# Constant matmuls ahead of five waits on TensorE, and a later X+U on GpSimd, in a 16-batch hybrid layer

## The reference

```python
x = x + attention(layernorm(x), Wqkv, Wproj)        # 16 heads of 16, rotary embedding, causal softmax
x = x + ffn(layernorm(x), weight, bias)             # blocks of 32 rounded to an FP6 E2M3 grid, then x @ W.T + bias
x = x + mamba_and_mlp(layernorm(x), ...)            # see below
x = x + ffn(layernorm(x), weight, bias)
```

## Time and profile before

| what | value |
|---|---|
| median of 3 runs | 9802.93 us (9801.65 to 9804.70) |
| the profiled execution | 9804.51 us |
| its span (first to last instruction) | 9802.8 us |
| mean granted TensorE clock | 0.909 |
| PE busy | 7878.8 us (80%) |
| DVE busy | 7618.6 us (78%) |
| POOL busy | 4330.9 us (44%) |
| ACT busy | 4259.3 us (43%) |

### The profile page before, as it was taken

One profiled execution on the slowest core, in us unless ns is written; L12 is line 12 of the kernel. 1 busy time (PEld: TensorE's weight loads), 2 busy tenths in 40 slices (PEclk: granted clock), 3 DMA queues, 4 the chain that ended last, 5 costly groups with the idle time before them and its releaser, 6 DMA issues. The chain is left out here.

```text
span 9802.8 us, 98275 instructions
## 1 busy us (share of the span) xinstructions
PE 7878.8 (80%) x31796; PEld 3811.3 (39%) x31796; DVE 7618.6 (78%) x11589; ACT 4259.3 (43%) x7991; POOL 4330.9 (44%) x2631
## 2 busy tenths in 40 slices
PE   5788787887978878788887878878788787887977
PEld 2343343433434334343343434434343243432434
DVE  5787977779687696876878778787787877878777
ACT  2535435254442543525435254353534535345353
POOL 1451825418154271632726336262361724518245
PEclk8898998989989898898989889899898988989989
DMA  3020020200202002020020200102011020100202
GB/s 78 1 51 3 5 49 1 52 1 9 45 0 53 1 9 45 0 53 1 13 41 0 53 1 22 32 0 53 1 28 26 0 53 1 38 15 5 49 1 52
DMA packets 265191, 229.93 MB, mean 23 GB/s; under 512 B 26947, under 2 KB 237635, under 8 KB 264531
## 3 DMA queue, kind: packets, MB, share of 16 engines
q1 hardware_dynamic: 264678, 223.50, 10.6%
HBM read 151.60 MB, written 70.25 MB: 23 GB/s over the span
## 5 line engine op out<-in xcount | busy, mean ns | idle before, releaser
L639 POOL TENSOR_TENSOR arena<-arena 128x1024 f32<-128x1024 f32 x1024 | 2435.6, 2389 | 1312.4 <-DVE arena L1041 862.4
L778 ACT ACTIVATE PS<-arena,Aneg 128x512 f32<-128x512 f32 x2048 | 1410.5, 691 | 1628.1 <-DVE XNT L1081 883.6
L704 ACT ACTIVATE arena<-PS 128x512 f32<-128x512 f32 (+3 forms) x3072 | 1286.9, 508 | 861.4 <-PE PS L1249 856.9
L1363 PE MATMUL PS<-XNT,identf 128*128 128x512 f32 x2048 | 1012.2, 618 | 320.9 <-POOL XNT L622 320.9
L948 DVE TENSOR_REDUCE pm<-PS 128x1 f32<-128x512 f32 (+3 forms) x1728 | 1051.2, 663 | 271.5 <-PE PS L1228 169.6
L601 POOL TENSOR_SCALAR_AFFINE_SELECT arena<-arena 128x512 f32<-128x512 f32 x512 | 329.6, 644 | 2063.6 <-ACT arena L704 2063.6
L1225 PE MATMUL PS<-arena 96*128 96x512 bf16 (+3 forms) x3072 | 1105.5, 385 | 106.3 <-PEq L1447 49.4
L1363 PE MATMUL PS<-arena,identf 128*128 128x512 f32 x2048 | 1025.6, 625 | 161.9 <-DVE arena L1057 161.9
L1249 PE MATMUL PS<-arena 99*128 99x512 bf16 (+3 forms) x3072 | 894.5, 332 | 5.9
L1348 PE MATMUL PS<-arena,sel 96*128 96x512 bf16 x1664 | 513.7, 391 | 389.0 <-DVE arena L1057 319.5
L686 ACT ACTIVATE XNT<-PS 128x512 f32<-128x512 f32 x320 | 187.4, 597 | 1335.2 <-PE PS L1184 1334.5
(11 more groups left out here) (143 smaller groups left out, 13086.2 us busy)
## 6 DMA issues: line engine op xcount, KB each, us to landing
pieces_scratch<-arena SPq DMA_DIRECT2D x816, 64.0 KB
arena<-pieces_scratch SPq DMA_DIRECT2D x68, 384.0 KB, 10.0
arena<-pieces_scratch SPq DMA_DIRECT2D x85, 256.0 KB, 10.5
arena<-in_x SPq DMA_DIRECT2D x17, 1024.0 KB, 5.6
U<-in_x SPq DMA_DIRECT2D x17, 1024.0 KB, 5.6
arena<-pieces_scratch SPq DMA_DIRECT2D x136, 128.0 KB, 10.2
out<-X SPq DMA_DIRECT2D x64, 256.0 KB, 5.7
arena<-pieces_scratch SPq DMA_DIRECT2D x17, 768.0 KB
```

Of the source, the lines that this page charges most:

```text
L639: nc.gpsimd.tensor_tensor(DB[:, n % 2], DTU[:, j, half(th)].unsqueeze(1).to_broadcast([P, SP2, TH]), BB[:, SP2 * sg:SP2 * (sg + 1), :], AL ...
L704: A(PT[s % len(PT)][:, hh, 0:w], bank(t_bank(n))[:, 0:w], ACT.Exp, scale=DH ** -0.5)\
L778: A(bank(da_bank(m)), DT[:, j, half(th)], ACT.Exp, scale=Aneg[:, j, SP2 * sg + ss:SP2 * sg + ss + 1]).then_inc(S("dA"), 1)
L1363: ins = MM(bank(4 + jt % 2), identf[:, :], HS[k % len(HS)][:, ss, :], start=False, stop=sg == NSG - 1 and ss == SP2 - 1)
```

## The change

`keep_busy(b, count)` issues `count` matmuls of the constants `identf` (the 128 x 128 identity, as weights) and `wproj[:, 0, :]` (256 columns) into bank b. Nothing reads what they write: the next use of the bank starts it anew. They stand ahead of waits in five places: the half `th` = 1 of both quantized layers (10 and 14 of them), ahead of `turn(2)` (5), ahead of x_proj's third and fourth `xc` (4 and 3), and in steps 0 and 1 of the scan loop (6, 2 and 4). Together that is 48 per batch, 96 matmul instructions. On POOL, X+U gets one more wait, `fxn` >= 8, the last of `front_norm`'s tiles.

```diff
             pool.wait_ge(S("R"), 2 * NT)
+            pool.wait_ge(S("fxn"), NT)
             nc.gpsimd.tensor_tensor(X[:, :, :], X[:, :, :], U[:, :, :], ALU.add).then_inc(S("xu"), 1)
...
+            def keep_busy(b, count):
+                for _ in range(count):
+                    MM(bank(b)[:, 0:C], identf[:, :], wproj[:, 0, :], start=True, stop=True)
...
             def quant_products(f):
                 rnd = (1, 4)[f]
                 for th in range(NTH):
+                    if th:
+                        keep_busy(NT // NTH, (10, 14)[f])
                     turn(rnd, lambda p, tt: quant_rows(f, p)[:, tt, :], "xd", lambda p: f * NT // 2 + p + 1,
...
+            keep_busy(7, 5)
             turn(2, lambda p, tt: RM[0][2 * p + tt], "R", lambda p: 2 * p + 2)
...
                 for j in range(ND):
+                    if th == 0 and j >= 2:
+                        keep_busy(5, (4, 3)[j - 2])
                     pe.wait_ge(S("xc"), j + 1)
...
                     jt, th, j, sg = m_unit(n)
+                    if n < 2:
+                        keep_busy(5, (6, 2)[n])
                     if b_copied(n + 1):
                         spread_b(b_copied(n + 1))
+                    if n == 1:
+                        keep_busy(5, 4)
                     if spread_c(n):
```

## The result

| | before | changed |
|---|---|---|
| median | 9803.77 us (4 runs) | 9586.55 us (4 runs, 9584.89 to 9598.34) |
| ratio | | 0.978, 95% interval 0.977 to 0.980 |
| profiled execution, its span | 9804.5, 9802.8 us | 9585.7, 9583.9 us |
| mean granted clock | 0.909 | 0.937 |
| PE busy | 7878.8 us | 7974.4 us |

The kernel is 217 us faster; 9606 us were forecast, with a range of 9560 to 9690. The 1536 added matmul instructions are all in the trace, and PE's busy time rises by 96 us only: the rest of its work runs faster.

A forecast was written before the change was run, and what follows sets the result against it. No engine was full; PE at 0.50 on chains and X+U's collision with `front_norm` cost time. Terms 1.3 + 1.3 + 0.6 + 2.4 + 5.1 + 1.8 = 12.5 us, taken as 12.3, over sixteen passes: 197 us, 9606 us; range 9560 to 9690.

The forecast's parts named there:

- The low clock lies on chains: At six places PE's clock falls to 0.50 while another engine soon waits for PE; half the covered low time comes back.
- the prediction's three sights: Low clock follows PE's idle time; another engine soon waits for PE in all six places; X+U and `front_norm` collide.
- X+U: On POOL, X+U waiting for `front_norm` removes PE's 3.53 us wait and the low stretch behind it: 5.1 us a pass.
- rival (d): X+U blocks DVE's silu products instead of the norm; its 5.1 us are lost, 9685 us; chance 0.05.
- The loop's block ends late: In the scan loop the block behind the wait for `z` is 1.1 us too long; 0.2 us charged.
- PE's waits for `xd`: Sign in the profile after: PE waits 1 us or less for `xd` ahead of the quantized layers' second halves.
- First quantized layer, -1.3 us: Ten constant matmuls, 4.3 us, fill an idle time of 5.17 us ahead of the second half's turn: 1.3 us a pass.
- rival (b): Low stretches shift as passes shorten; half of the clock's 7.4 us is given back, 8.8 us a pass, 9662 us; chance 0.20.
- The last block's 1.9 us: Second quantized layer: 28 instructions fill 7.09 us of idle time, keeping the pass's last chain at 1.00; forecast 1.8 us.
- the loop's 2.4 us: Scan loop's blocks remove its low stretch: 2.6 us less 0.2 us for lateness; bounds -2.3 and +4 us.
- (a): Only X+U pays, since the constants would not hold the clock: 82 us gained, 9721 us; chance 0.09.
- (c): Blocks start at 0.50, take twice as long and delay queued work: 13.2 us a pass slower, 10014 us; chance 0.04.

The follow-up runs named there:

- X+U alone: Changed kernel without its constant matmuls, keeping only X+U's wait for the norm: 9693.6 us, ratio 0.989 to the kernel before.
- The kernel with 15: Changed kernel with 15 instead of 10 constant matmuls ahead of the second half of the first quantized layer: 9583.3 us, ratio 0.978 to the kernel before.
- a delay of 2.1 us: Changed kernel with two constant fills of 1024 columns on DVE ahead of the first quantized layer: 9643.5 us, 57 us more than the changed kernel.
- dt_proj at 128 rows: Changed kernel with dt_proj's weights zero-padded from 16 to 128 rows: 9572.2 us; with 15 instead of 10 matmuls in the first block too: 9582.1 us.
- the constants alone: Changed kernel with all constant matmuls but without X+U's added wait: 9668.9 us, ratio 0.986 to the kernel before.
- doubled blocks: Changed kernel with every block of constant matmuls twice as long: 9805.4 us, ratio 1.000 to the kernel before.

## Why the prediction was right, point by point

**The low clock lies on chains.** Right. Five of the six stretches at 0.50 went, and the chains behind them shortened as the terms said, by half of the low time covered less the waits that stay: 1.3, 0.6, 2.4 and 1.9 us, each within 0.1 us of its term. That the block did it is shown for the loop and for the end of the pass, where the low clock came back without it. For 1.3 and 0.6 us, at `turn(2)` and x_proj, it is argued only: with X+U alone the clock was 1.00 there too. The first of the prediction's three sights, that the low clock follows idle time, is a habit of these traces and not a rule: 1.95 us of idle time were followed by it before, 1.96 us at the same place with X+U alone were not.

**X+U.** Right, and sized right: 5.4 us against 5.1 in the stage. `front_norm` takes 2.67 us for 6.48, PE goes on without a wait. L1107 starts at 9480.28 beside X+U (9479.21 to 9483.75) and L1107's longest call of all is 690 ns, so rival (d) is out:

```profile
L1107 DVE SCALAR_TENSOR_TENSOR arena<-arena,PS x256: 677/687/690, 614.4 to 9515.1; 128x512 f32<-128x512 f32 x128
```

**The loop's block ends late.** Right: charged 0.2 us, ACT waits 0.16 us. B's spread starts 5.44 us behind the start of `z` (9238.04 - 9232.60), against 4.25 us before: 1.2 us later, where 1.1 were said. By the letter this is one of the prediction's own signs of a wrong forecast, a block that ends over 1 us after its wait was met in most passes; the sign was badly set, since the sum had counted on it. The idle time ahead of the block (1.6 us in this trace, 2.0 in the prediction) did not bring the clock down here, though 1.95 us did elsewhere; that was left to luck in the prediction and stays unexplained by it.

**PE's waits for `xd`.** The sign asked for 1 us or less ahead of the second halves; they are 2.41 and 1.81 us. At the first the low clock came, at the second it did not.

**First quantized layer, -1.3 us.** Wrong in size: no gain (3.94 against 3.90 us). The step that failed is "an idle time of 5.17 us", read from before and held fixed. In the changed kernel the low stretch at the first half's products ends earlier against the work, they take 4.19 us instead of 5.74, and the same block leaves 2.4 us. The kernel with 15 shows it in the passes of its first kind.

**dt_proj, no term.** A gain of 2.1 us that the sum did not have. Its low stretch was in the trace of before (9422.9), and the prediction put it at nothing without a reason. It was touched: it began 5.2 us behind the first of the 16 matmuls instead of 3.0 and was 3.4 us shorter, and the 16 took 9.0 us instead of 11.1. Why it moved so was not tried.

**The terms as a sum.** The total, -13.7 against -12.5 us, came out near because 1.3 us that did not come and 2.1 us that nobody had counted nearly cancel; that part is luck. As a principle the sum is weak, and rival (b) named why: when a pass shortens, the low stretches fall elsewhere in it. Its price did not come (9662 us; the shift gave a little instead of taking half), its mechanism did, in both directions. The last block's 1.9 us cost 0.1 us when taken away, the loop's 2.4 us cost 4.3, a delay of 2.1 us cost 3.8, and filling the first wait wholly gained nothing clear of noise, alone or with dt_proj at 128 rows.

**Rivals.** (a) is out: the constants alone give 132 us. (c) is out for this change (the clock was 1.00 ahead of the blocks), but a late block costs nearly what it said: with doubled blocks 13.7 us a pass came of 15.7 expected, and the whole gain is given back.

**What stays open.** Five kernels have a mean pass of 590.4 to 590.6 us. In three of them the passes repeat to 0.2 us once the first few are over, in the changed kernel they lie within 0.7 us, and with 15 in the first block two lengths alternate about that mean. The kernel before and the one with doubled blocks repeat at 604.2 us, X+U alone at 597.3 us; some others wander by up to 7 us. This was seen and not tried by itself. A reading that fits, and that no run tests: the place of the low stretches in a pass depends on the pass before, and the pass's length on their place; a fixed length is where the two agree.

## What to carry to other kernels

Where PE waits a few us and its next work is on a chain, count at most half of the low stretch behind the wait as lost, and fill the wait with constant work that ends just before it is met; too long a filler costs nearly its whole overhang. Do not add up single gains in a looped kernel of this kind to better than a few us a pass, and judge each filler again once the others are in: here one was worth nothing, one nearly twice its term. Look for ops whose collision makes one engine stand behind a long instruction of another; moving X+U behind eight short ones cost nothing and gave 107 us alone.

## What the hardware showed that was not expected

- Matmuls with 16 rows let the clock fall to 0.50 while PE was busy 11.8 of 13.5 us (kernel before); padded to 128 rows, the same matmuls kept 1.00 in all 16 passes and took 7.03 us, for 9.0 in the changed kernel and 11.1 before.
- Alternating narrow and full matmuls stayed at 0.50 for 23 us with PE busy for 22.7 of them.
- Float32 transposes by the identity held the clock like matmuls: 9587.5 against 9586.6 us.
- Idle times of the same length were followed by the low clock at one time (1.95 us, kernel before) and not at another (1.96 us, X+U alone).
- Passes of different kernels share a mean length (590.5 us in five, 604.2 us in two), and small edits showed nothing or nearly twice their size.
